# Feed-forward weights in stationary order, first scales spread by TensorE, rows normalised in two parts, passage to attention interleaved

## The reference, cut to what matters

```python
# x: (4, 256, 512) float32; attention: 32 query heads, 8 key/value heads of 128, window of 128
xn = layernorm(x)
s = (rope'd, windowed attention of xn with wq, wk, wv) @ wo
W1, W3 = dequant(w1, s1), dequant(w3, s3)     # each (1376, 512)
W2 = dequant(w2, s2)                          # (512, 1376)
g = silu((silu(xn @ W1.T) * (xn @ W3.T)) @ W2.T)
out = x + s * g

def dequant(w, s):   # w: int32, each holds one packed byte = two signed 4-bit values
    msb, lsb = w >> 4, ((w & 15) ^ 8) - 8
    g = concatenate([msb, lsb], axis=1).reshape(-1, 64)   # groups of 64 with one scale each
    return g * s[:, None]
```

## Time and profile before

| | |
|---|---|
| median of 3 runs | 873.5 us (873.45 to 874.37) |
| the profiled execution | 874.13 us, of which the instructions span 872.3 us |
| PE busy | 840.8 us, 96% of the span |
| VectorE busy | 597.1 us, 68% |
| ScalarE busy | 472.3 us, 54% |
| GpSimd busy | 390.2 us, 45% |
| moved by DMA | 32.55 MB |

### The profile page before, as it was taken

How to read it: one execution, slowest core, us unless ns; L and a number is a source line. 1 busy time by engine, 2 the same in 40 slices (tenths; PEclk the granted TensorE clock), 3 DMA queues, 4 the chain that set the end, 5 groups by cost and what they waited for, 6 DMA issues and landing times.

```text
span 872.3 us, 13995 instructions
## 1 busy us (share of the span) xinstructions
PE 840.8 (96%) x4252; PEld 702.3 (81%) x4252; DVE 597.1 (68%) x1615; ACT 472.3 (54%) x1139; POOL 390.2 (45%) x303
## 2 busy tenths in 40 slices
PE   3999999999989999999999999999999999999987
PEld 3777888888767888888888888888888888888876
DVE  7953554433569676876868596777759686866794
ACT  2474121132667557574757575475747566664742
POOL 0144121124545536551744454275525545641893
PEclk9999999999999999999999999999999999999989
DMA  6200001002010201200120102012001201100121
GB/s 195 57 15 10 12 25 46 24 1 72 1 31 19 74 0 49 65 10 1 48 72 0 48 19 54 0 48 72 0 4 44 72 0 48 49 23 0 49 62 72
DMA packets 40224, 32.55 MB, mean 37 GB/s; under 512 B 5056, under 2 KB 32384, under 8 KB 40192
## 3 DMA queue, kind: packets, MB, share of 16 engines
q1 hardware_dynamic: 40192, 32.16, 13.0%
HBM read 30.05 MB, written 2.10 MB: 37 GB/s over the span
## 4 chain that ended last, share of the span: by engine, by line
PE 86%; DVE 6%; ACT 3%; issue 2%; POOL 2%; DMA 0%; SPq 0%; ACTq 0%; DVEq 0%; POOLq 0%
PE bank L982 26%; PE bank L984 25%; PE bank L983 25%; PE bank L1122 5%; PE bank L1102 3%; DVE probs L831 1%; ACT W2raw L434 1%; POOL acc L338 1%; PE bank L1092 1%; PE bank L1002 1%; DVE xl L667 1%; POOL swap L321 1%; DMA xn<-in_L_attn_x 0%; POOL q L325 0%; ACT W2h L435 0%
## 5 line engine op out<-in xcount | busy, mean ns | idle before, releaser
L321 POOL TENSOR_TENSOR swap<-swap,cst 128x512 f32<-128x512 f32 x80 | 103.7, 1296 | 251.1 <-ACT swap L489 249.8
L982 PE MATMUL bank<-xh,wih 128*128 128x512 f32 x384 | 158.0, 411 | 0.2 <-DVE q L795 0.2
L984 PE MATMUL bank<-xh,wil 128*128 128x512 f32 x384 | 150.7, 393 | 0.0
L983 PE MATMUL bank<-xl,wih 128*128 128x512 f32 x384 | 150.0, 391 | 0.0
L516 ACT ACTIVATE probs<-probs,nmx 128x128 f32<-128x128 f32 (+1 forms) x256 | 113.5, 444 | 36.5 <-DVE nmx L816 36.1
L831 DVE TENSOR_SCALAR probs<-probs,rinv 128x128 f32<-128x128 f32 x250 | 125.4, 544 | 4.4
L532 ACT ACTIVATE ph<-bank 128x512 fp32r<-128x512 f32 x96 | 55.7, 598 | 109.5 <-PE bank L1122 108.1
L982 PE MATMUL bank<-woh,oh 128*128 128x512 f32 x256 | 101.1, 395 | 0.0
L983 PE MATMUL bank<-wol,oh 128*128 128x512 f32 x256 | 100.5, 393 | 0.0
L984 PE MATMUL bank<-woh,ol 128*128 128x512 f32 x256 | 100.5, 393 | 0.0
L287 POOL TENSOR_TENSOR hl<-act_h,hh 128x512 fp32r<-128x512 f32 x22 | 29.9, 1363 | 148.1 <-ACT hh L417 148.1
(11 more groups left out here) (103 smaller groups left out, 1832.3 us busy)
## 6 DMA issues: line engine op xcount, KB each, us to landing
raw<-in_L_attn_wq SPq DMA_DIRECT2D x32, 256.0 KB, 2.9
raw<-in_L_attn_wo SPq DMA_DIRECT2D x32, 256.0 KB, 2.9
packed<-in_L_ffn_w SPq DMA_DIRECT2D x20, 128.0 KB, 2.1
xn<-in_L_attn_x SPq DMA_DIRECT2D x8, 256.0 KB, 3.4
raw<-in_L_attn_wk SPq DMA_DIRECT2D x8, 256.0 KB, 3.0
raw<-in_L_attn_wv SPq DMA_DIRECT2D x8, 256.0 KB, 2.6
raw<-in_L_attn_x SPq DMA_DIRECT2D x8, 256.0 KB, 2.8
out<-gate SPq DMA_DIRECT2D x8, 256.0 KB, 2.0
```

What stands on the lines that cost most here:

```text
L321: nc.gpsimd.tensor_tensor(v, v, spread(sin.unsqueeze(1), P, 2, SEQ), ALU.mult).then_inc(sin_done, 1)
L982: nc.tensor.matmul(out_, sh, mh, start=(i == 0), stop=False)
L983: nc.tensor.matmul(out_, sh, ml, start=False, stop=False)
L984: m = nc.tensor.matmul(out_, sl, mh, start=False, stop=(i == n - 1))
```

## The change

- **Layout.** The host hands over w1/w3 (`w13`) with the model dimension already on the partition, and w2 (`w2`) with the hidden unit on it; codes of both nibbles come in one array, two halves of the partitions (or four columns of a group) read the same byte and pick their nibble by a shift count (`shc`). Scales come spread out (`s13`, `s2`), w1/w3's spread over 64 partitions by the load. All transposes of weights go, and so do the loops: all 11 tiles are written out.
- **First scales.** For tiles 0 and 1 the scales come as two rows, and TensorE spreads them over the partitions into PSUM (`scale_rows`: four matmuls of 2 rows by 512 columns, plain fp32).
- **Normalisation.** In each half of the rows some tiles are normalised by VectorE (0, 2, 3; 4, 6) and some by ScalarE (1; 5, 7). Tiles 0 and 1 of the hidden width run half 0 of the rows first for both, then half 1.
- **Banks.** `w2_mult` goes round four banks (7, 6, 1, 0) instead of two.
- **Passage.** Pair 4 and the single tile 10 of `w2_mult` are split in halves of four row tiles and put between the `project`s; `gates` is split likewise on ScalarE; scores wait for all reads of `ffn_add`.

```diff
@@ loads (SP; the first scales, shift counts and identity from ScalarE's queue)
+            def load13(t, m):
+                wait(sp, W13_done, 2 * t + m - 3)
+                s = t % 2
+                for half in range(2):
+                    rows = slice(half * HALF, half * HALF + HALF)
+                    sp.dma_start(pk[rows, s, m, :], w13[:, t, m, :]).then_inc(w13_in[s][m], 16)
+                    if t > 1:
+                        sp.dma_start(sc[rows, s, m, :], s13[half, t, m:m + 1, :].to_broadcast([HALF, PK])) \
+                            .then_inc(w13_in[s][m], 16)
+            def load2(t):
+                wait(sp, W2_done, t - 1)
+                sp.dma_start(pk2[:, t % 2, :], w2[t]).then_inc(w2_in[t % 2], 16)
+                sp.dma_start(sc2[:, t % 2, :], s2[t]).then_inc(w2_in[t % 2], 16)
+            load13(0, 0)
             for i in range(4):
                 load_x(i)
-            sp.dma_start(cst[:, :], const).then_inc(const_in, 16)
+            load13(0, 1)
+            load13(1, 0)
             for i in range(4, NT):
                 load_x(i)
+            load13(1, 1)
+            for t in range(2, FT):
+                for m in range(2):
+                    load13(t, m)
+                if t == 2:
+                    sp.dma_start(cst[:, 0:C_ID], const[:, 0:C_ID]).then_inc(const_in, 16)
+                load2(t - 2)
@@ GpSimd
+            for t in range(2):
+                for m in range(2):
+                    w13_first(t, m)          # low part of W13, tiles 0 and 1
+            hid_lo(0, 0); hid_lo(1, 0); hid_lo(0, 1); hid_lo(1, 1); w2_lo(0)
+            for t in range(2, FT):
+                hid_lo(t, 0); w2_lo(t - 1); hid_lo(t, 1)
@@ ScalarE
+            act.dma_start(sfirst[:, :, :, :], s13[:, 0:2, :, :]).then_inc(sfirst_in, 16)
+            act.dma_start(sides[:, :], side).then_inc(sfirst_in, 16)
+            act.dma_start(shc[:, :], shifts).then_inc(shift_in, 16)
+            act.dma_start(ident, const[:, C_ID:C_ID + P]).then_inc(id_in, 16)
+            w13_hi(0, 0)
+            root(0)
+            norm(1)
+            for i in range(4):
+                x_hi(i)
+            w13_hi(0, 1)
+            w13_hi(1, 0)
+            root(1)
+            w13_hi(1, 1)
+            norm(5)
+            norm(7)
...
             halves(0, 0, 0)
             v_out(0, 0)
             halves(0, 0, 1)
+            kq_hi(0, 0, 0)
             v_hi(0, 0, T_B[1])
+            gates(range(4))
+            halves(0, 0, 2)
+            kq_hi(0, 0, 1)
+            halves(0, 0, 3)
+            gates(range(4, NT))
+            kq_hi(0, 0, 2)
+            halves(0, 0, 4)
@@ VectorE
+            def dequant13(t, m):
+                dve.wait_ge(w13_in[s][m], 64 * (t // 2) + 32)
+                if t < 2:
+                    dve.wait_ge(sfirst_ps, 2 * t + m + 1)
...
+                nc.vector.tensor_scalar(nib[:, m, :], pk[:, s, m, :], shc[:, 4:5], shc[:, 5:6],
+                                        ALU.logical_shift_left, ALU.arith_shift_right).then_inc(nib_done, 1)
+                scale = bank[2 + 2 * t + m][:, :] if t < 2 else sc[:, s, m, :]
+                nc.vector.tensor_tensor(W13[:, m, :], nib[:, m, :], scale, ALU.mult).then_inc(W13_done, 1)
+            def dequant2(t):
+                nc.vector.tensor_tensor(nib2.., pk2.., spread(shc[:, 0:4].unsqueeze(1), P, P, 4), ALU.logical_shift_left)
+                nc.vector.tensor_scalar(nib2[:, :], nib2[:, :], 28, None, ALU.arith_shift_right)
+                nc.vector.tensor_tensor(W2[:, s, :], nib2[:, :], sc2[:, s, :], ALU.mult).then_inc(W2_done, 1)
+            dve.wait_ge(shift_in, 16)
+            dequant13(0, 0)
+            for i in range(4):
+                stats(i)
+            scales(0)
+            norm_here(0); norm_here(2); norm_here(3)
+            x_lo(0); x_lo(1)
+            dequant13(0, 1)
+            x_lo(2); x_lo(3)
+            dequant13(1, 0)
+            for i in range(4, NT):
+                stats(i)
+            scales(1)
+            norm_here(4); norm_here(6)
+            dequant13(1, 1)
+            x_lo(4); x_lo(5); hid(0, 0); x_lo(6); x_lo(7)
...
+            for t in range(2, FT):
+                dequant13(t + 2, 0); hid(t, 0); dequant13(t + 2, 1)
+                dequant2(t - 1); hid(t, 1)
+                w13_lo(t + 2, 0); w13_lo(t + 2, 1)
+                if t > 2 and t % 2:
+                    ffn_add((t - 3) // 2)
@@ PE
+            pe.wait_ge(sfirst_in, 32)
+            scale_rows(0, 0)
+            scale_rows(0, 1)
+            pe.wait_ge(id_in, 16)
+            for i in range(4):
+                x_turn(i)
+            scale_rows(1, 0)
+            scale_rows(1, 1)
+            w13_start(0, 0)                 # 12 matmuls of 256 columns, row tiles 0 and 1
+            w13_start(0, 1)                 # 12 of 256 columns, row tiles 2 and 3
+            w13_mult(0, 0, 1)
+            w13_mult(1, 0, 0, {3: lambda: x_turn(4)})
+            for i in range(5, NT):
+                x_turn(i)
+            w13_mult(1, 0, 1)
+            for t in range(2):
+                w13_mult(t, 1, 0)
+                w13_mult(t, 1, 1)
+            w13_tile(2)
+            for u in range(FT // 2 - 1):
+                w13_tile(2 * u + 3)
+                w2_mult(u, (0, 1))
+                w13_tile(2 * u + 4)
+            w2_mult(FT // 2 - 1, (0, 1), range(4))
             project(0, 0, 0)
             project(0, 0, 1)
-            w2_mult(FT // 2, (0,))
+            w2_mult(FT // 2 - 1, (0, 1), range(4, NT))
             project(0, 0, 2)
+            w2_mult(FT // 2, (0,), range(4))
             v_turn(0, 0, T_B[1])
+            project(0, 0, 3)
+            w2_mult(FT // 2, (0,), range(4, NT))
+            project(0, 0, 4)
+            project(0, 0, 5)
+            pe.wait_ge(ffn_read, 6 * NT)
             scores(0, 0, 0, 0)
```

More of the change, by code:

```diff
@@ L176, in cnt, with part_of, turn @@
             return 2 * per * g + (per * bp + c)
+        PARTS = ((0, 1, 2, 3), (4, 5, 6, 7))
+        def part_of(i):
+            return [i in tiles for tiles in PARTS].index(True)
+        def turn(t, half):
+            return 2 * half + t if t < 2 else 2 * t + half
         def second(ap):
@@ L632, in _, with stats, scales @@
         def _(dve):
-            def small(i, part, fn, *args):
-                dve.wait_ge(ln_small, 6 * part + i)
-                fn(*args).then_inc(ln_small, 1)
-            def statistics(part):
-                tiles = range(4 * part, 4 * part + 4)
-                for i in tiles:
-                    dve.wait_ge(x_in[i], 16)
-                    nc.vector.bn_stats(stat[:, i, :], xn[:, i, :]).then_inc(stats_done, 1)
+            def stats(i):
+                dve.wait_ge(x_in[i], 16)
+                nc.vector.bn_stats(stat[:, i, :], xn[:, i, :]).then_inc(stats_done, 1)
+            def scales(part):
+                tiles = PARTS[part]
+                first, last = tiles[0], tiles[-1] + 1
                 for i in tiles:
@@ L724, in ffn_add @@
+            def ffn_add(u, tiles=range(NT)):
+                for i in tiles:
                     dve.wait_ge(ffn_ps, 8 * u + (i + 1))
-                    src = bank[7 - i % 2][:, :]
-                    if isinstance(u, int) and u == 0:
+                    src = bank[F_B[i % 4]][:, :]
+                    if u == 0:
                         nc.vector.tensor_copy(gate[:, i, :], src).then_inc(ffn_read, 1)
@@ new lines, in w13_mult @@
+            def w13_mult(t, half, m, ahead=None):
+                n, s = turn(t, half), t % 2
+                wait(pe, h_done, n - 1)
+                if t < 2:
+                    pe.wait_ge(xl_done, 4 * half + 4)
+                    pe.wait_ge(W13l_first, 2 * t + m + 1)
+                else:
+                    pe.wait_ge(W13l_done, 2 * t + m - 3)
+                cols = slice(half * IT, half * IT + IT)
+                three(bank[2 + 2 * (n % 2) + m][:, :],
+                      [(W13h[:, s, m, d, :], W13l[:, s, m, d, :], xh[:, d, cols], xl[:, d, cols])
+                       for d in range(DT)], ahead).then_inc(ab_ps, 1)
@@ new lines, in w13_start, with w13_tile @@
+            def w13_start(m, part):
+                cols = slice(2 * part * P, (2 * part + 2) * P)
+                pe.wait_ge(W13l_first, m + 1)
+                pe.wait_ge(xl_done, 2 * part + 2)
+                i = three(bank[2 + m][:, cols],
+                          [(W13h[:, 0, m, d, :], W13l[:, 0, m, d, :], xh[:, d, cols], xl[:, d, cols])
+                           for d in range(DT)])
+                if part:
+                    i.then_inc(ab_ps, 1)
+            def w13_tile(t):
+                for half in range(2):
+                    for m in range(2):
+                        w13_mult(t, half, m)
@@ new lines, in w2_mult @@
+            def w2_mult(u, pair, tiles=range(NT)):
+                pe.wait_ge(W2l_done, 2 * u + len(pair))
+                pe.wait_ge(hl_done, 4 * u + 2 * len(pair))
+                for i in tiles:
```

(5 more changed lines are left out.)

581 lines of the change are left out of this document (249 added, 332 removed).

## The result

The changed kernel takes 860.41 us (median of 4 executions, 855.81 to 861.75), the kernel before 873.58 us (4 executions on the same chip, 873.45 to 874.37): ratio 0.9839, 95% interval 0.9818 to 0.9861. It is 13.2 us faster, where 19.4 were forecast. The profiled execution took 861.75 us with a span of 859.9, 7.0 more than the 852.9 forecast.

A forecast was written before the change was run, and what follows sets the result against it. PE, busy 96% of the span, was taken as the bound; 7.2 + 6.9 + 1.2 + 1.6 + 2.5 + 0 = 19.4 us less gave a median of 854.1 us, bounds 851 to 858, whole range 849 to 862.

The forecast's parts named there:

- the collisions: Rival: VectorE's two-SBUF steps take 1.79 us beside GpSimd, PE stands 0.7 us in nine tiles; 858 to 866, chance 0.09.
- Turns of w1/w3 and w2: Feed-forward weight transposes on PE all go: 7.2 us for w1/w3 and 6.9 us for w2.
- the waits tied to them: Feed-forward body: two PE losses of 0.6 us each, tied to the weight turns, go; 1.2 us.
- the restarts behind transposes: Feed-forward matmuls: the first block behind transposes costs 0.1 us more, at 16 interrupted places; 1.6 us go.
- The head: Start of feed-forward, where PE waits: fourth block of 12 matmuls ends at 30.7 us instead of 33.2, gain 2.5.
- the sign that I named for the head: The head forecast is wrong if VectorE's first statistics start before 5 or after 9 us.
- The body's other engines: Per hidden tile VectorE needs some 9.8 us, up to 13.1 with collisions, under PE's 16.4; nothing late, cost nothing.
- The passage: Feed-forward to attention: four banks and interleaving gain 1.2 us, ScalarE's gates give 1.2 back; net 0.
- Transfers: Rival: loads of 1.5 MB per hidden tile become the bound, time not less than before; chance 0.05.
- Small loads late: Rival that the head gives nothing: small loads land after x tiles and hold VectorE; 857.5 us, chance 0.12.
- Transposes hidden: Rival: weight transposes were hidden under matmuls, so removal gives only the waits; about 868 us, chance 0.02.
- Attention carried over: From the turn of the first probabilities on, code is the same; its 623.5 us stay unchanged.

The follow-up runs named there:

- the priced kernel: Changed kernel plus, behind `w13_tile(2)`, four unused spreading matmuls of 2 rows, then 24 matmuls of 256 columns and 24 of 512: 868.85 us, one execution.
- the fillers: Changed kernel plus unused matmuls, 5 ahead of the first spreading matmul and 9 behind the second, to keep PE at work: 857.07 us, ratio 0.9812.
- the fastest kernel: Changed kernel plus 5 and 9 unused matmuls, pair 0's first four adds ahead of W13's low parts, and late second gates: 852.42 us, ratio 0.9753.

## Why the prediction was right in direction and 6 us too good

The measured median, 860.41, lies in the whole range of 849 to 862, but outside the 851 to 858 that I gave the forecast with its bounds: it stands where I had put the collisions, 858 to 866.

*Turns of w1/w3 and w2, the waits tied to them, the restarts behind transposes (16.9 us).* Right. Not one PE row reads the identity against weights; doubling the transposes cost 0.09 us each; after pair 0, PE has no wait in the body, and its 96 matmuls between pairs take 21.80 us. The sum closes: from the end of the fourth block to the first scores it was 204.9 us before (33.3 to 238.16) and 190.3 after, 14.6 less; without pair 0's loss of 4.3 that is 18.9, of which 1.2 are the passage's and 0.8 the faster body's: 16.9.

*The head (forecast: gain 2.5).* Wrong in the profiled execution, by 3.7: a loss of 1.2. The failed step is a size in PE's list: I took the spreading matmul at 0.9 us and narrow ones at 0.147. Both prices are near the right ones at full rate (0.93 and 0.12 in the body of the priced kernel), but in the head PE ran them at half rate, 1.85 and 0.213: 1.9 us for the two later spreading matmuls and 1.6 for the 24 narrow ones. The x turns, also slow, were not mis-sized, because their price came from the head before, where the 16 took 3.44 us too; they end at 15.44, forecast 15.4. VectorE's list came out near the forecast, its first statistics at 7.08 us (7.3) and its first norm at 11.18 (11.5), but by luck: the small loads had landed at 3.68 and not at 5.7 to 6.1, and the slow spreading matmul and VectorE's wait for it (until 5.90) took most of that back. So the sign that I named for the head, statistics before 5 or after 9 us, stayed silent while the head was wrong. Where PE comes to full rate early, half 1 starts at 31.2, near the 30.7 forecast, and that is where the other lists put it: in the three profiles of the kernels up to the fillers in which they and not PE's rate are the bound it starts at 30.8 to 31.4, for the 30.6 I gave them.

*The body's other engines (forecast: nothing late, cost nothing).* Wrong, and the largest miss; its sign, PE idle for `ffn_add` after 35 us, came. The step that failed is "PE needs 16.4 us per hidden tile", a mean over tiles with and without `w2_mult`. Tiles 2 and 3 follow each other with no `w2_mult` between, so PE gives 10.9 us for each. VectorE's steps of 9.8 us would fit into that, but not with the waits for ScalarE among them (1.19 and 1.22 us) and a collision on top (1.80 instead of 0.69 for L737 at 66.43), and pair 0 is the first to want four banks at once with the adds at the end of VectorE's list. PE stood 2.4 us, and in the profiled execution the clock fell behind it, 1.9 more. The rival "collisions reach PE" named 860, but as nine tiles at 0.7 us; it was one place at 4.3, in which the collision is some 1.1 by the estimate above, and no run takes the collision alone away. That the rival's number came out near is luck. L737 took 14.2 us in its 11 runs, 0.68 us the shortest and 1.80 the longest, so about six of them collided; after pair 0 none of it reached PE.

*The passage (forecast: net 0, turn 11.9 us behind the last project).* Right within 0.3: 11.6, so net 0.2. The 1.2 gained by four banks show in `w2_mult`'s quarters of 24 at 5.45 us, the loss in the gates, of which moving the second behind the last copy gave back 1.0.

*Other rivals.* Transfers: DMA moved 105 GB/s in the body and PE never waited for a load after the first 3.7 us; refuted. Small loads late: PE had its rows at 3.68 us, and VectorE's first step, at 5.90, waited for PE and not for a load; refuted. Transposes hidden: refuted by the doubling. Attention carried over at 623.5: 623.6.

## What to carry to other kernels

Where a sum says "this engine has 16 us per tile and needs 13", find the stretch where the bounding engine goes fastest through a tile and lay the lists beside each other there; the mean hides it, and the cure may be one call moved in one list. Small matmuls early in a program are to be priced from rows of the same stretch, since the same instruction took twice as long in the head as in the body; and where a kernel's executions spread, compare two profiles of the same code before looking for a cause in the change.

## What the runs showed of the hardware that I had not expected

- In one execution the granted clock fell to 0.78 during four plain fp32 matmuls with 2 rows in use and to 0.55 behind them, while PE was busy all the time; with 128 rows, in one execution, it stayed at 1.00. Behind two such matmuls in the head it fell to 0.50 in two profiles and not in two others.
- The granted clock of a stretch can read 1.00 while PE works at half rate: in the first 16 us of the profiles here 16 x turns took 3.4 to 3.6 us, or 1.9 behind fillers, both with 1.00 in that column. The column missed narrow matmuls at 0.213 us between 19.15 and 24.44 us of the kernel after, and showed those of 17.1 to 20.5 us in the fastest kernel as 0.50; the spacing of starts told the rate in both.
- The same wait of 2.4 us was followed by a clock of 0.58 in one execution and of 1.00 in another of the same kernel; over the five profiles that have it, by the lower clock in two.
